# TensorE's loops over the pairs in attention and in the last stage, and the order of down products and up projection

## The reference

```
attn = sliding_attn(src, src, src, w=32)        # 16 heads of 8, window 3*32
x1 = ln(src + attn) * g1 + b1
x2 = ln(x1 + relu(x1 @ W1 + b_1) @ W2 + b_2) * g2 + b2
x  = ln(src + x2)
q  = batchnorm(x @ w_q)                         # statistics over all tokens
sim = q . keys                                  # 2 halves x 8 heads x 32 keys
top 8 of each half, top 8 of their 64 sums      # picks 8 of 1024 experts a head
h  = softmax(scores) * gelu(x . down_embed[picked])
out = ln(x + sum(h * up_embed[picked]))
```

## Time and profile before

| | us |
|---|---|
| median of 3 runs | 668.64 (667.21 to 670.53) |
| profiled run, its time | 669.26 |
| its span, first to last instruction | 667.4 |
| TensorE busy in the span | 528.7 (79%) |
| VectorE busy | 541.9 (81%) |
| ScalarE busy | 410.6 (62%) |
| GpSimd busy | 401.9 (60%) |
| mean granted TensorE clock | 0.946 of full |

### The profile page before, as it was taken

One profiled execution on the slowest core, in us unless ns is written; L12 is line 12 of the kernel. 1 busy time (PEld: TensorE's weight loads), 2 busy tenths in 40 slices (PEclk: granted clock), 3 DMA queues, 4 the chain that ended last, 5 costly groups with the idle time before them and its releaser, 6 DMA issues.

```text
span 667.4 us, 42223 instructions
## 1 busy us (share of the span) xinstructions
PE 528.7 (79%) x17863; PEld 446.7 (67%) x17863; DVE 541.9 (81%) x1741; ACT 410.6 (62%) x813; POOL 401.9 (60%) x520
## 2 busy tenths in 40 slices
PE   0376899999997899995547788888888888888865
PEld 0265788888886576775336777776776677677755
DVE  5655698898987478864789988999999999999961
ACT  4344577777775457774164766667766776677562
POOL 7443356556652136442167786787878787877760
PEclk9978899999998999996699988999999999999897
DMA  6776576755426010100012232332233323332330
GB/s 213 229 236 197 166 235 191 195 168 189 158 68 241 18 33 17 32 0 1 9 44 56 66 79 52 72 75 67 55 79 75 71 51 79 75 74 50 70 76 10
DMA packets 44934, 64.60 MB, mean 97 GB/s; under 512 B 5456, under 2 KB 37072, under 8 KB 42320
## 3 DMA queue, kind: packets, MB, share of 16 engines
q1 hardware_dynamic: 44880, 63.84, 34.5%
HBM read 36.29 MB, written 8.65 MB: 67 GB/s over the span
## 4 chain that ended last, share of the span: by engine, by line
PE 48%; issue 19%; ACT 12%; POOL 10%; DVE 7%; DMA 1%; POOLq 1%; ACTq 0%; SPq 0%; DVEq 0%
PE ps L750 9%; PE ps L765 5%; PE ps L730 5%; PE ps L811 5%; PE ps L917 4%; ACT early L1061 4%; PE ps L824 4%; ACT tile_rows L1073 4%; PE ps L938 3%; PE ps L740 3%; POOL tile_rows L659 2%; PE ps L926 2%; PE ps L776 2%; PE ps L902 2%; POOL rstd L686 2%
## 5 line engine op out<-in xcount | busy, mean ns | idle before, releaser
L917 PE MATMUL ps<-arena,hid 128*32 128x32 f32 x8192 | 82.5, 200 | 35.6 <-issue 22.0
L959 ACT ACTIVATE arena<-ps 128x512 f32<-128x512 f32 x128 | 70.2, 595 | 62.8 <-PE ps L750 62.8
L917 PEld LDWEIGHTS ps<-arena,hid 128*32 128x32 f32 x8192 | 77.5, 113 | 42.5 <-issue 28.7
L938 PE MATMUL ps<-up_sb,prod 128*128 128x128 f32 x512 | 70.7, 294 | 24.6 <-DVE prod L1434 24.6
L938 PEld LDWEIGHTS ps<-up_sb,prod 128*128 128x128 f32 x512 | 65.4, 204 | 29.2 <-DVE prod L1434 29.2
L1166 DVE TENSOR_REDUCE row_max<-ps 128x8 f32<-128x768 f32 x64 | 61.0, 953 | 19.5 <-PE ps L740 19.4
L750 PE MATMUL ps<-ident,arena 128*128 128x128 f32 x512 | 72.8, 290 | 1.1 <-issue 1.1
L750 PEld LDWEIGHTS ps<-ident,arena 128*128 128x128 f32 x512 | 63.7, 151 | 2.8 <-issue 1.7
L1169 DVE TENSOR_TENSOR arena<-ps,row_max 128x768 f32<-128x768 f32 x64 | 61.3, 958 | 5.1 <-DVE row_max L1166 0.2
L665 POOL TENSOR_TENSOR wq_sb<-wq_sb,tile_rows 128x1024 f32<-128x1024 f32 x32 | 64.7, 2022 | 0.8 <-DVE wq_sb L1410 0.6
L926 PE MATMUL ps<-xT,downT_sb 128*128 (+1 forms) x512 | 62.9, 277 | 0.0
(11 more groups left out here) (159 smaller groups left out, 1347.5 us busy)
## 6 DMA issues: line engine op xcount, KB each, us to landing
arena<-r_x SPq DMA_DIRECT2D x128, 128.0 KB
early<-terms SPq DMA_DIRECT2D x8, 720.0 KB
xT<-terms SPq DMA_DIRECT2D x8, 720.0 KB
hid<-terms SPq DMA_DIRECT2D x8, 720.0 KB
prod<-terms SPq DMA_DIRECT2D x8, 720.0 KB
x_pair<-in_x_wrapped SPq DMA_DIRECT2D x16, 256.0 KB, 2.8
x<-in_x SPq DMA_DIRECT2D x8, 256.0 KB, 2.8
xT_tile<-xT SPq DMA_DIRECT2D x32, 64.0 KB, 1.9
```

The lines of the kernel that those rows point to most:

```text
L917: mm = nc.tensor.matmul(slots[32 * g:32 * g + 32, k, c], leftT[p][:, r // 2, r % 2, :], blocks_of[p][:, :, r // 2, r % 2, GROUP * g:GROUP ...
L938: mm = nc.tensor.matmul(ps[:, 6 + p, 0:P], pairs[:, c // 2, c % 2], up_sb[:, c, :], start=False, stop=(c == EC - 1))
L959: return nc.scalar.activation(out_ap, in_ap, ACT.Copy)
```

## The change

TensorE's attention loop runs over all 16 pairs, with no pair written out. For that its waits have to be met in the first pair too, and its steps have to exist in the first and last tile: counts are shifted by initial increments (`r1_done`, `norm_done` and `pt_copied` by 2), the attention output is also computed for a tile -1, from zeros, and the scores for a tile 32, from what lies in the buffers. GpSimd sets those zeros at the start, increments `rows_ready` by 2 at the end of its part, and clears 256 more columns that are added to `xT`. In the last stage TensorE writes out the pairs -1 and 0 and loops over 1 to 15; only the up projection of tile 31 follows. In that loop the similarities are computed for tiles 32 and 33 and the down products for tile 32, whose results nobody reads, and SyncE loads the two tiles' columns. And in each tile the down products of t+1 stand ahead of the up projection of t-1. The other engines keep their loops.

```diff
-        xT = sb("xT", [P, W + tokens + W])
+        xT = sb("xT", [P, tokens + 2 * P])
...
         edge_ready = sem("edge_ready")
         probs_cleared = sem("probs_cleared")
+        heads_cleared = sem("heads_cleared")
         scores_done = sem("scores_done")
...
                 for p in range(2):
                     t, o = 2 * i + p, 1 - p
-                    if have(t + 3):
+                    if not isinstance(t, int) or -3 <= t < NT - 1:
                         x_columns(t + 3, o)
...
             nc.gpsimd.memset(eps_col[:], EPS).then_inc(eps_ready, 1)
             nc.gpsimd.memset(zeros[:], 0.0)
+            nc.gpsimd.memset(xT[:, tokens:tokens + 2 * P], 0.0)
+            nc.gpsimd.memset(heads_out[1][:], 0.0).then_inc(heads_cleared, 1)
             for q in range(2):
...
                 p, u = k % 2, (k // 2) % 2
                 pool.wait_ge(edge_ready, t + 1)
-                need(pool, r1_done, t - 1)
+                pool.wait_ge(r1_done, t + 1)
                 hold(pool)
...
             copy_rows(2, 0, 2)
             over_pairs(pool, NQ, b1_operands)
+            pool.sem_inc(rows_ready, 2)
...
                 pe.wait_ge(exp_done, 2 * t + half + 1)
                 if half == 0:
-                    need(pe, r1_done, t - 1)
+                    pe.wait_ge(r1_done, t + 1)
                 for g in (2 * half, 2 * half + 1):
-                    need(pe, pt_copied, GROUPS * t + g - 1)
+                    pe.wait_ge(pt_copied, GROUPS * t + g + 1)
                     for b in range(BLOCKS):
...
                     pe.wait_ge(edge_ready, t + 2)
                 values_of = [v_edge[p], v_mid[p], v_mid[p], v_edge[1 - p]]
-                need(pe, norm_done, 2 * (t - 1) + half + 1)
+                pe.wait_ge(norm_done, 2 * t + half + 1)
                 for g in (2 * half, 2 * half + 1):
-                    pe.wait_ge(pt_copied, GROUPS * t + g + 1)
+                    pe.wait_ge(pt_copied, GROUPS * t + g + 3)
                     for b in range(BLOCKS):
...
             def attn_out(t, p, copied):
-                pe.wait_ge(norm_done, 2 * t + 2)
-                pe.wait_ge(pt_copied, copied)
+                pe.wait_ge(norm_done, 2 * t + 4)
+                pe.wait_ge(pt_copied, copied + 2)
                 for h in range(4):
...
                 mm.then_inc(attn_done, 1)
-            def b1_pe(i, first, last):
+            def b1_pe(i):
                 for p in range(2):
                     t = 2 * i + p
                     following = (t + 1, i + p, 1 - p)
-                    more = not (last and p == 1)
-                    if more:
-                        scores(*following, 0)
+                    scores(*following, 0)
                     probs_transpose(t, p, 0)
-                    if more:
-                        scores(*following, 1)
+                    scores(*following, 1)
                     probs_transpose(t, p, 1)
                     values(t, p, 0)
-                    if not (first and p == 0):
-                        attn_out(t - 1, 1 - p, GROUPS * t + 3)
+                    attn_out(t - 1, 1 - p, GROUPS * t + 3)
                     values(t, p, 1)
+            pe.wait_ge(heads_cleared, 1)
             for half in range(2):
                 scores(0, 0, 0, half)
-            over_pairs(pe, PAIRS, b1_pe)
+            with pe.Fori(0, PAIRS) as i:
+                b1_pe(i)
...
-            pe.wait_ge(r1_done, NT)
+            pe.wait_ge(r1_done, NT + 2)
...
                 for p in range(2):
                     t, o = 2 * i + p, 1 - p
-                    if have(t + 2):
+                    if not isinstance(t, int) or t >= -2:
                         similarities(t + 2, p, i + 1)
+                    if not isinstance(t, int) or t >= -1:
+                        down(t + 1)
                     if have(t - 1):
                         up_projection(t - 1, o)
-                    if have(t + 1):
-                        down(t + 1)
                     if have(t):
                         outer(t, p, i)
-            over_tiles(pe, d_pe)
+
+            for i in (-1, 0):
+                d_pe(i)
+            with pe.Fori(1, PAIRS) as i:
+                d_pe(i)
+            up_projection(NT - 1, 1)
...
         @block.scalar
         def _(a):
+            a.sem_inc(pt_copied, 2)
+
             def copy(out_ap, in_ap):
...
             def stage(n, q):
-                a.wait_ge(r1_done, 4 * n + 4)
+                a.wait_ge(r1_done, 4 * n + 6)
                 need(a, y1_done, n - 1)
...
             V.tensor_copy(row_heads[:], stretch(fold4[:, 0:1], P))
+            v.sem_inc(r1_done, 2)
+            v.sem_inc(norm_done, 2)
+
             def split_x(c):
...
                 v.wait_ge(norm_step, n + 1)
                 if half == 0:
-                    need(v, attn_done, t - 1)
+                    need(v, attn_done, t)
                 V.tensor_tensor(heads_out[p][:, 2 * half:2 * half + 2].rearrange("p g b d -> p (g b) d"), pv[:, :, 0:DH],
...
             def residual(t, p):
-                v.wait_ge(attn_done, t + 1)
+                v.wait_ge(attn_done, t + 2)
                 v.wait_ge(mid_ready, t + 1)
...
```

## The result

| | before | after |
|---|---|---|
| median of 4 runs of each, side by side | 669.59 (667.21 to 671.26) | 650.79 (647.67 to 651.51) |
| profiled run, its time | 669.26 | 650.28 |
| its span | 667.4 | 648.5 |
| mean granted clock of TensorE | 0.946 | 0.96 |
| packets of the instruction queue q8 | 39 | 18 |

The ratio is 0.970 (0.966 to 0.974): 20 us less, by the profiled runs 19. The span's saving falls to the stages as follows. Each line is the start of the group named, on TensorE.

What follows compares the result with a forecast made beforehand. TensorE bounds attention, a ScalarE-GpSimd chain the steady last stage; elsewhere TensorE waits for code. Terms 8.8 - 0.4 + 0 + 1.5 + 0 + 7.8 save 17.7 us: 651.6 profiled, 650.9 median, 80% range 643 to 660.

Steps and rivals of the forecast that it cites:

- What bounds: TensorE bounds steady attention; the last stage's chain runs over ScalarE and GpSimd; "issue" stalls are TensorE waiting for code.
- it does not do what it says: Rival 5: a loop body is not kept and stalls in every pass; nothing saved, 668 us, chance 0.01.
- Attention, entry: Pair 0 becomes the loop's first pass, pair 1 finds code loaded: slot 7 8.8 us earlier, bounds 3 and 12.
- Start: Start of attention: GpSimd's two new fills ahead of the row clears cost 0.4 us on the path.
- Attention between: Attention's slots 7 to 30: 5.105 us each as before; possibly late row transfers of tile 12 charged nothing.
- Attention, exit: End of attention: 4.55 us stall goes, but TensorE waits for GpSimd's last increment; taken as 0, bounds -1.5 to +2.4.
- Last stage, entry: Start of last stage: straight pair 1 and its first-pass loss go; saves 1.5 us, bounds 0.5 and 3.5.
- Order: Last stage, down products before up projection: wait moves to before the outer products, tile stays 9.5 us, gain 0.
- Tail: End of last stage: straight pairs 14 and 15 and their stalls go; saves 7.8 us, bounds 5 and 9.
- Rivals 3 and 4: 3: new order frees VectorE, 643.5 us, chance 0.06; 4: merged idle time costs TensorE's clock, 671 us, chance 0.03.
- Rivals 1 and 2: 1: attention gives little, 659 us, chance 0.14; 2: tail gives 4 us instead of 7.8, 655 us, chance 0.12.
- rival 1: Attention's two terms come to 1 us instead of 8.5; saving 10, 659 us, chance 0.14.

Runs made afterwards that it cites:

- the stores of the entry: Changed kernel with SyncE's three late store groups issued behind rows of pairs 2, 4 and 6 instead of 1, 3 and 4: 651.78 us, ratio 0.971.
- the three edits together: Changed kernel with rows_ready released early, last store group one pair later, two new fills behind the row clears: 648.81 us, ratio 0.967.

## Why the prediction was right, and where it was off

Predicted 650.9, measured 650.79; for the profiled run 651.6, measured 650.28. The near hit is in part luck: terms that were too small and losses that were not charged cancelled, and several terms differ between traces by more than they missed.

- **What bounds.** Right. "issue" stalls are TensorE waiting for code: packets fell from 39 to 18, the stalls of the removed copies went, and larger bodies brought them back. The rival "it does not do what it says" falls with the empty instruction queue.
- **Attention, entry, 8.8 predicted, 10.9 measured.** The term was mis-sized in its assumption that slot 2 would run at the lower clock, as in the trace of before. It took 5.0 us, not 8.2. Against that pair 0 took 19.1 us instead of 17.9 + 0.7. Why the clock came back early is not shown. The near reading, that two short stalls spare it and one long one does not, is refuted by other traces: with the same attention code the first stall was 3.69 us in the second trace of after and 6.70 us in that of two pairs a pass in the last stage, and slot 2 took 5.0 us in both, while the last stage's loop alone had 2.49, 1.52 and 2.63 us and stood at the lower level from 43 to 59 us. Slot 2 took 6.2 to 6.5 us in the traces of attention alone, of the stores of the entry and of the three edits together. Slot 7 began at 84.0, 86.0 and 88.9 us in the three traces with the old attention loop and between 74.0 and 79.0 in those with the new one (the doubled body left out), so a term read from one trace of each is good to 2 us or so.
- **Start, -0.4 predicted, -0.3 measured.** Right.
- **Attention between, 0 predicted, -2.8 measured.** The prediction named the transfer and charged nothing, because it is issued behind work that moves. It moved by less. That explains 1.1 us. The rest, most of it 0.11 us a pair at the attention output of the second tile, was not foreseen, and its cause is open. It is the largest step that failed.
- **Attention, exit, 0 predicted, 1.7 measured.** Inside its bounds of -1.5 to 2.4. The stated mechanism came: TensorE waits for GpSimd, then runs some microseconds at the lower clock. But the size is not firm: with the same wait the exit took 12.9 to 15.6 us in eight traces, by the clock behind it, and with the old loop 16.1 in before and 14.3 in the run of the order alone.
- **Last stage, entry, 1.5 predicted, 1.4 measured** with the steady tiles. One trace can't carry this number: the same code took 262.4 us from tile 0 to tile 27 in the trace of before and 265.7 in that of attention alone.
- **Order, 0 predicted.** Right in each part: the up projection's wait gone, 1.6 to 1.8 us before the outer products (1.5 said), the period unchanged, and 0.2% at most in the run of it alone. Rivals 3 and 4 both fall: VectorE's idle time did not go, and the gap did not bring the clock down in one of the 20 tiles read.
- **Tail, 7.8 predicted, 8.6 measured.** Tile 30 to 31 took 7.51 us (7.6 said). The difference is the 0.7 us kept for a code stall that did not come: the code behind the loop is one short up projection.
- **Rivals 1 and 2** (attention or the tail gives little) did not come (rival 1 has 8.5 where the two terms, with the start, add up to 8.4), though in the run of the last stage's loop alone the time gained was 2 us less than its tail.

## What to carry over

A stall marked "issue" at the first pass of a body, together with packets on the instruction queue, is code being loaded; a written-out first or last iteration costs that once each, and folding it into the loop is worth more than the few products of nobody's tile that it adds (here 20 us for about 6 us of them: similarities 2 x 1.1, down products 1.95, scores of tile 32 and attention output of tile -1 about 1.7). Before a body is made larger, count its records: this change gained 3% by removing copies, and doubling the body of the same loops lost 7 and 24% against the kernel before. When the chain of waits does not pass the engine whose wait moves, as with the order here, count the move as nothing from the start.

## What the runs showed of the hardware

- A loop body of 1172 TensorE records stays loaded over the 14 passes behind the first, with no packet of q8 from 395 us on. One of 1952 records is fetched whole in every pass, about ten packets of 16 KB, with single stalls up to 5.1 us and 20.5 us in one pass of 45.6.
- Beside the stalls of a body that does not stay, the granted clock fell to 0.76 (attention) and 0.87 (last stage) of full.
- The length of one stall does not tell how long the lower clock lasts. In attention's first passes it lasted from 43 to 56 us after 3.92 us (before), from 43 to 59 after 2.49 (last stage's loop alone), but only from 43 to 46 after 3.69 (after, second trace) and from 42 to 48 with one of 6.70 (two pairs a pass in the last stage). The same wait of 2.73 us at the end of attention was followed by the lower level in six traces and by the full clock in two. A gap of 1.6 to 1.8 us in every tile left it at 1.00 for 210 us.
- Code stalls differ between runs of the same code. In attention they add up to 11.2 us in the trace of before, 12.5 in that of the order alone and 13.0 in that of the last stage's loop alone, whose attention code on TensorE is the same; the loops with the old order, run twice, had 3.64 and 0.35 us in pair 0 once and 3.69 and 1.53 the other time. With the new attention loop kept, the first stall of pair 0 measured from 1.48 us (attention alone) to 6.70 (two pairs a pass in the last stage). A term of 1 or 2 us in such a place can't be read from a single trace.
